# Routed experts of a transformer block: fp32 matmuls become three fp32r products with split weights

## The reference

```python
scores = sigmoid(x @ router_weight.T)
topk_indices = _get_topk_indices(scores, e_bias)      # best 2 groups of 4, then best 2 experts
combine = zeros((T, 16)).at[arange(T)[:, None], topk_indices].add(topk_weights)
h1 = einsum('th,ehi->tei', x, w_up)                   # 512 -> 256, each expert
a = relu2(h1) * combine[:, :, None]                   # relu(h) squared
routed = einsum('tei,eih->th', a, w_down)             # 256 -> 512
shared = relu2(hidden @ shared_up) @ shared_down
```

## Time and profile before

| | us |
|---|---|
| median of 3 runs (2376.22 to 2377.37) | 2376.26 |
| profiled execution | 2383.18 |
| its span | 2381.4 |
| PE busy | 1936.1 (81%) |
| PEld busy | 1183.5 (50%) |
| DVE busy | 1152.1 (48%) |
| ACT busy | 761.1 (32%) |
| POOL busy | 610.8 (26%) |

### The profile page before, as it was taken

How to read it: one execution, slowest core, us unless ns; L and a number is a source line. 1 busy time by engine, 2 the same in 40 slices (tenths; PEclk the granted TensorE clock), 3 DMA queues, 4 the chain that set the end, 5 groups by cost and what they waited for, 6 DMA issues and landing times. The chain is left out here.

```text
span 2381.4 us, 34828 instructions
## 1 busy us (share of the span) xinstructions
PE 1936.1 (81%) x9788; PEld 1183.5 (50%) x9789; DVE 1152.1 (48%) x2951; ACT 761.1 (32%) x1215; POOL 610.8 (26%) x743
## 2 busy tenths in 40 slices
PE   4888887888887888887888876999999759999900
PEld 0644433644434544435544324767777636666600
DVE  3355544345643455633556528555555223333358
ACT  1345452245452255533344513222222112222200
POOL 0201116111125011143011144554444421000064
PEclk8889998899998899998799997999999979999955
DMA  6222203222302222312322223222222186333388
GB/s 212 54 54 54 50 23 99 53 54 54 72 5 95 54 54 54 72 46 79 64 44 43 56 92 121 97 94 93 84 84 89 66 309 229 127 128 128 113 296 309
DMA packets 104973, 232.52 MB, mean 98 GB/s; under 512 B 20440, under 2 KB 20440, under 8 KB 104812
## 3 DMA queue, kind: packets, MB, share of 16 engines
q1 hardware_dynamic: 81008, 171.86, 25.2%
q0 software_dynamic: 14848, 50.34, 5.8%
q10 hardware_dynamic: 8960, 8.41, 1.1%
HBM read 113.06 MB, written 67.17 MB: 76 GB/s over the span
## 5 line engine op out<-in xcount | busy, mean ns | idle before, releaser
L402 ACT ACTIVATE pr<-sc 128x1024 f32<-128x1024 f32 (+3 forms) x384 | 307.9, 811 | 263.2 <-PE sc L641 261.3
L661 PE MATMUL O<-pr,V 128*32 128x512 f32 (+3 forms) x3072 | 325.6, 498 | 42.6 <-ACT oD L414 42.6
L328 POOL TENSOR_SCALAR_AFFINE_SELECT pr<-pr 128x256 f32<-128x256 f32 x256 | 103.4, 409 | 969.7 <-ACT pr L402 969.7
L504 DVE TENSOR_REDUCE mx<-ring 128x1 f32<-128x512 f32 x256 | 169.6, 678 | 246.2 <-PE ring L616 244.5
L500 DVE CUSTOM_DVE_ANT_0 ring<-ring,mask 128x512 f32<-128x512 f32 (+3 forms) x512 | 240.8, 511 | 62.7 <-PE ring L616 60.4
L641 PE MATMUL sc<-stk 128*128 128x512 f32 (+3 forms) x768 | 241.6, 396 | 23.0 <-ACT pr L402 20.9
L641 PEld LDWEIGHTS sc<-stk 128*128 128x128 f32 x768 | 115.7, 189 | 262.5 <-ACT pr L402 155.3
L616 PE MATMUL ring<-stk 96*128 96x512 f32 (+3 forms) x768 | 218.0, 388 | 20.0 <-DMA stk<-st 13.1
L616 PEld LDWEIGHTS ring<-stk 96*128 96x128 f32 x768 | 144.6, 204 | 68.2 <-DVE mx L500 17.6
L529 DVE RECIPROCAL oD<-oD 128x128 f32<-128x128 f32 x128 | 117.6, 934 | 93.1 <-ACT oD L414 93.1
L1519 PE MATMUL ue<-wu_e,xT_e 128*128 x632 | 151.2, 383 | 0.1
(11 more groups left out here) (228 smaller groups left out, 3396.1 us busy)
## 6 DMA issues: line engine op xcount, KB each, us to landing
stk<-st SPq DMA_DIRECT2D x192, 256.0 KB, 5.0
x_e<-xs SPq DMA_DIRECT2D x79, 256.0 KB, 2.6
ys<-y_e SPq DMA_DIRECT2D x79, 256.0 KB, 2.0
oT<-in_L_attn_x_dram ACTq DMA_DIRECT2D x16, 512.0 KB, 5.6
st<-in_L_attn_x_dram SPq DMA_DIRECT2D x32, 256.0 KB, 3.2
x1d<-pr SPq DMA_DIRECT2D x32, 256.0 KB, 2.1
xb<-x1d SPq DMA_DIRECT2D x32, 256.0 KB, 2.9
part<-y_sh SPq DMA_DIRECT2D x32, 256.0 KB, 2.0
```

The source lines that it names most:

```text
L402: nc.scalar.activation(pr[:, g % PRB, :, off:], sc[g % 2][:, :, off:], ACT.Exp, scale=SCALE).then_inc(exp_done, 1)
L504: nc.vector.tensor_reduce(mx[:, heads[0]:heads[-1] + 1, qt, part], bank[:, 0:len(heads) * w].rearrange("p (e k) -> p e k", e=len(heads)), ...
L661: last = nc.tensor.matmul(O[row:row + 32, off:], V[:, col:col + DH], pr[:, g % PRB, e, off:], start=(i == 0), stop=(i == 4 * c + 3))
```

## The change

The expert stage goes from plain fp32 to the three-pass product. GpSimd now fetches an expert's weights into one of three raw buffers, copies them rounded to fp32r into one of eight places (`WR`), and subtracts to get the low part; hi and lo lie next to each other, so that one up matmul of 512 columns gives x_hi times both, and one of 256 columns adds x_lo times w_hi. The ninth and later experts wait for their place by the count of finished tiles (`endi`). ScalarE makes the high parts and now also copies the cross term and the result; VectorE makes the low parts, adds the cross term, and does relu and square in one instruction. The wait for the weights moves from TensorE to VectorE, which loads the expert's count once a tile, with its check. TensorE loads an offset (`eslot`) without a check; the loop's first two rounds of four load two, the other two load one. Spare tiles now ask for expert 15 instead of expert 0. In the loads of the first three experts nothing waits for the zero rows any more.

```diff
+WR = 8
+RAW = 3
-        xT = sb("xT_e", [P, 2, KC, P])
+        xhi, xlo = sb("xhi_e", [P, 2, KC, P], f32r), sb("xlo_e", [P, 2, KC, P], f32r)
...
+            def split(e):
...
+                pool.wait_ge(raw_in[z], (e // RAW + 1) * 32)
+                if e >= WR:
+                    done = pool.value_load(endi[0:1, e - WR:e - WR + 1], min_val=1, max_val=NET + 1)
+                    pool.wait_ge(d_done, done)
+                    apart(pool)
+                nc.gpsimd.tensor_copy(up[:, :, 0, :], up_raw).then_inc(whi_ready, 1)
+                nc.gpsimd.tensor_copy(dn[:, :, 0, :], dn_raw).then_inc(whi_ready, 1)
+                pool.wait_ge(whi_ready, 2 * e + 2)
+                nc.gpsimd.tensor_tensor(up[:, :, 1, :], up_raw, up[:, :, 0, :].bitcast(f32), ALU.subtract).then_inc(w_ready, 1)
+                nc.gpsimd.tensor_tensor(dn[:, :, 1, :], dn_raw, dn[:, :, 0, :].bitcast(f32), ALU.subtract).then_inc(w_ready, 1)
+            for e in range(RAW):
+                fetch(e)
+            for e in range(E):
+                if e == WR:
+                    pool.wait_ge(tables, 1)
+                split(e)
+                if e + RAW < E:
+                    pool.wait_ge(w_ready, 2 * e + 2)
+                    fetch(e + RAW)
...
         @block.scalar
...
-                    nc.scalar.activation(r[:, s % 2, :], ub[s % 2][:, 0:EI], ACT.Relu).then_inc(r_ready, 1)
+                    nc.scalar.activation(cross[:, s % 2, :], ub[s % 2][:, EI:2 * EI], ACT.Copy).then_inc(cross_ready, 1)
+                if has(j + 1 if known(j) else j):
...
+                    nc.scalar.activation(ahi[:, (s + 1) % 2, :, :], tab[(s + 1) % 2][:, 0:EC * P].rearrange("p (k t) -> p k t", k=EC), ACT.Copy).then_inc(ahi_ready, 1)
+                if has(j):
...
+                    nc.scalar.activation(y[:, s, :], db[s % 2][:, :], ACT.Copy).then_inc(y_ready, 1)
...
         @block.vector
...
+                if has(j + 3 if known(j) else j):
+                    split = dve.value_load(eid[0:1, j + 3:j + 4] if known(j) else eid[0:1, bass.ds(j + 3, 1)], min_val=2, max_val=2 * E)
+                    dve.wait_ge(w_ready, split)
+                    apart(dve)
+                    dve.wait_ge(xhi_ready, j + 4)
+                    nc.vector.tensor_tensor(xlo[:, z, :, :], txb[z][:, :, :], xhi[:, z, :, :].bitcast(f32), ALU.subtract).then_inc(xlo_ready, 1)
+                    nc.vector.tensor_tensor(h1[:, :], ub[s % 2][:, 0:EI], cross[:, s % 2, :], ALU.add).then_inc(h1_ready, 1)
+                    nc.vector.scalar_tensor_tensor(a[:, s % 2, :], h1[:, :], 0.0, h1[:, :], ALU.max, ALU.mult).then_inc(a_ready, 1)
+                    nc.vector.tensor_tensor(alo[:, z, :, :], tab[z][:, 0:EC * P].rearrange("p (k t) -> p k t", k=EC),
+                                            ahi[:, z, :, :].bitcast(f32), ALU.subtract).then_inc(alo_ready, 1)
...
         @block.tensor
...
-                return pe.value_load(K.eid[0:1, t:t + 1] if known(t) else K.eid[0:1, bass.ds(t, 1)], min_val=0, max_val=E - 1)
+                return nc.values_load(at, engines=[mybir.EngineType.PE], min_val=0, max_val=(WR - 1) * SLOT,
+                                      skip_runtime_bounds_check_because="the table holds multiples of SLOT below WR * SLOT")
+                if has(j + 2 if known(j) else j):
+                    slot[s + 2] = offset(j + 2)
+                    w = slot[s + 2]
+                if has(j):
+                    w_down = slot[s] if s >= 2 else offset(j)
-                    e = expert(j + 2)
-                    pe.wait_ge(w_ready, e + 1)
-                        last = nc.tensor.matmul(ub[s % 2][:, 0:EI], xT[:, s % 2, k, :], K.wu[:, bass.ds(e * (KC * EI) + k * EI, EI)],
-                                                start=(k == 0), stop=(k == KC - 1))
+                        both = lambda: nc.tensor.matmul(ub[s % 2][:, :], xhi[:, s % 2, k, :], part(wup, at, 2 * EI, w),
+                                                        start=(k == 0), stop=(k == KC - 1), skip_group_check=True)
+                        if k < KC - 1:
+                            both()
+                        nc.tensor.matmul(ub[s % 2][:, 0:EI], xlo[:, s % 2, k, :], part(wup, at, EI, w),
+                                         start=False, stop=False, skip_group_check=True)
+                        if k == KC - 1:
+                            last = both()
-                    for k in range(EC):
-                        last = nc.tensor.matmul(db[s % 2][:, :], aT[:, s % 2, k, :], K.wd[:, bass.ds(e * (EC * D) + k * D, D)],
-                                                start=(k == 0), stop=(k == EC - 1))
+                    terms = [(a_, h, k) for k in range(EC) for a_, h in ((ahi, 0), (ahi, 1), (alo, 0))]
+                    for n, (a_, h, k) in enumerate(terms):
+                        last = nc.tensor.matmul(db[s % 2][:, :], a_[:, s % 2, k, :], part(wdn, (2 * k + h) * D, D, w_down),
+                                                start=(n == 0), stop=(n == len(terms) - 1))
```

More of the change, by code:

```diff
@@ L1290, in expert_phase @@
         sem = lambda n: ctx.enter_context(nc.semaphore(n))
+        wup = sb("wup_e", [P, WR * KC * 2 * EI], f32r)
+        wdn = sb("wdn_e", [P, WR * EC * 2 * D], f32r)
+        raw = sb("raw_e", [P, RAW, WN])
         x = sb("x_e", [P, XR, D])
-        xT = sb("xT_e", [P, 2, KC, P])
-        r = sb("r_e", [P, 2, EI])
+        xhi, xlo = sb("xhi_e", [P, 2, KC, P], f32r), sb("xlo_e", [P, 2, KC, P], f32r)
+        cross = sb("cross_e", [P, 2, EI])
+        h1 = sb("h1_e", [P, EI])
         a = sb("a_e", [P, 2, EI])
-        aT = sb("aT_e", [P, 2, EC, P])
+        ahi, alo = sb("ahi_e", [P, 2, EC, P], f32r), sb("alo_e", [P, 2, EC, P], f32r)
         y = sb("y_e", [P, XR, D])
@@ L1313, in expert_phase @@
         base = sb("base", [P, E])
-        inside, other, mine_e = sb("inside", [P, E]), sb("other", [P, E]), sb("mine_e", [P, E])
-        rowf = sb("rowf", [P, 4])
+        inside, other = sb("inside", [P, E]), sb("other", [P, E])
+        rowf = sb("rowf", [P, 6])
         padf = sb("padf", [P, E])
@@ L1319, in expert_phase @@
         moved = sb("moved", [P, 2 * NTILE])
-        padi = sb("padi", [P, E], i32)
+        padi, endi = sb("padi", [P, E], i32), sb("endi", [P, E], i32)
+        eid, eslot, xrow = sb("eid", [P, NET], i32), sb("eslot", [P, NET], i32), sb("xrow", [P, NET], i32)
         iotas, zeroed, step, tables = sem("iotas"), sem("rows_zeroed"), sem("table_step"), sem("tables")
         in_columns, in_rows = sem("in_columns"), sem("in_rows")
-        w_in = [sem(f"we_in{i}") for i in range(2)]
-        w_ready, padded = sem("we_ready"), sem("padded")
+        raw_in = [sem(f"raw_e_in{i}") for i in range(RAW)]
+        whi_ready, w_ready, padded = sem("whi_e_ready"), sem("we_ready"), sem("padded")
         block = ctx.enter_context(nc.Block())
@@ L1464, in _ @@
             nc.vector.tensor_copy(padi[:, :], padf[:, :])
+            nc.vector.tensor_scalar(endi[:, :], ends[:, :], float(PRIMED), None, ALU.add)
             ts(inside[:, :], starts[:, :], jf[:, 0:1], None, ALU.is_le)
@@ L1468, in _ @@
             then(tt(inside[:, :], inside[:, :], other[:, :], ALU.subtract))
-            red(rowf[:, 0:1], inside[:, :], AX.X, ALU.add)
-            tt(other[:, :], inside[:, :], base[:, :], ALU.mult)
-            then(tt(mine_e[:, :], inside[:, :], ef[:, :], ALU.mult))
+            red(rowf[:, 2:3], other[:, :], AX.X, ALU.add)
+            then(red(rowf[:, 0:1], inside[:, :], AX.X, ALU.add))
+            then(ts(rowf[:, 2:3], rowf[:, 2:3], float(E - 1), None, ALU.min))
+            then(tt(other[:, :], inside[:, :], base[:, :], ALU.mult))
             red(rowf[:, 1:2], other[:, :], AX.X, ALU.add)
-            red(rowf[:, 2:3], mine_e[:, :], AX.X, ALU.add)
+            then(ts(rowf[:, 4:5], rowf[:, 2:3], float(WR), -float(WR), ALU.is_ge, ALU.mult))
+            then(tt(rowf[:, 4:5], rowf[:, 4:5], rowf[:, 2:3], ALU.add))
+            ts(rowf[:, 4:5], rowf[:, 4:5], float(SLOT), None, ALU.mult)
+            then(ts(rowf[:, 2:3], rowf[:, 2:3], 2.0, 2.0, ALU.mult, ALU.add))
             then(ts(rowf[:, 3:4], jf[:, :], float(P), None, ALU.mult))
@@ L1496, in _ @@
             pe.wait_ge(in_columns, 1)
-            for n in range(2):
+            for n in range(3):
                 last = nc.tensor.transpose(txb[0][0:1, n, 0:NET], rowf[0:NET, 2 + n:3 + n], K.ident[0:NET, 0:NET])
@@ L1500, in _, with offset, part @@
             pe.wait_ge(tables, 1)
-            def expert(t):
-                return pe.value_load(K.eid[0:1, t:t + 1] if known(t) else K.eid[0:1, bass.ds(t, 1)], min_val=0, max_val=E - 1)
-            def round_(j, s):
+            slot = {}
+            def offset(t):
+                at = eslot[0:1, t:t + 1] if known(t) else eslot[0:1, bass.ds(t, 1)]
+                return nc.values_load(at, engines=[mybir.EngineType.PE], min_val=0, max_val=(WR - 1) * SLOT,
```

(10 more changed lines are left out.)

87 lines of the change are left out of this document (44 added, 43 removed).

## The result

The changed kernel takes 2339.95 us (median of six runs, 2338.48 to 2341.45) against 2376.62 (2375.71 to 2377.92) for the kernel before beside it: ratio 0.9846, 95% interval 0.9833 to 0.9858, 36.7 us less. The forecast was 2331, range 2319 to 2354. The profiled execution took 2338.48 us, its span is 2336.7.

A forecast was written before the change was run, and what follows sets the result against it. TensorE's expert round was taken as the bound; 43.6 us from shorter rounds and 2 from the start took the profiled 2383.18 to 2337.6, or the 2376.26 median to 2330.7 us. Range 2319 to 2354.

The forecast's parts named there:

- The bound and the round: Expert stage: TensorE stays the bound, its round falls from 4.11 to 3.55 us, 42.8 us over 76 full rounds.
- the prediction's own signs: Signs of being right: TensorE rounds of 3.5 to 3.6 us without idle time, expert stage 284 us instead of 329.
- rival D: TensorE's fp32r matmuls run at column count alone: round 3.25 us, gain 68, 2308 us; chance 0.04.
- rivals A and B: TensorE's sequencer binds: A, round 3.83 us, 2353 us, chance 0.13; B, round 4.70, slower at 2421 us, chance 0.10.
- 1.8 us to spare: Expert rounds: ScalarE's and VectorE's results are ready some 1.8 us before TensorE wants them.
- rival C: VectorE's wait for weights near tile 7, GpSimd needing 15 us an expert: 2346 us; chance 0.06.
- Weights: GpSimd's splits take 9.5 us an expert and stay hidden: cost 0, at most 1 to 2 us at tile 7.
- The start: Expert stage's beginning: fewer weights beside the first x and a shorter ramp, net gain 2 us, bounds -1 and +5.
- The table's delay: Start of the expert stage: extra table steps on VectorE, a transpose and a cast make it 1.2 us later.
- the forecast's own: Whole kernel: the forecast's own range, 2320 to 2342 us, from round 3.44 to 3.69 and start -1 to +5; chance 0.67.

The follow-up runs named there:

- e_loads: Changed kernel with two checked register loads of the offset per tile on TensorE instead of one or two unchecked: 2348.58 us, ratio 0.9883.
- e_best2: Changed kernel with weight wait on TensorE, no VectorE load, ReLU on ScalarE, zero rows on two queues, fourth expert fetched later: 2327.81 us, ratio 0.9794.
- e_copies: Changed kernel with GpSimd making the weights' low parts by a second copy instead of a subtraction (values wrong): 2347.15 us, ratio 0.9851.

## Why the prediction was right, and where it was off

- **The bound and the round.** Right in kind: TensorE stays full, the round shrinks at each part. 3.46 us instead of the forecast 3.55: transposes in front of fp32r, 512 columns and the first product behind transposes came as taken from the earlier trace rows. Off were two small terms: 256 columns cost 0.12 and not 0.1275, and the two transposes 0.13 and not half of four (0.18). Over 76 rounds this is 6 to 7 us more gain; 2.7 of it went to what VectorE loses beside GpSimd. By the prediction's own signs the round lies just under its 3.5 to 3.6 us, and from first transposes to last down matmul the stage takes 280.8 us (forecast 284).
- **Fp32r at its column count alone (rival D)** fell: 512 columns cost 0.23.
- **TensorE's sequencer (rivals A and B)** fell: late rounds have no idle time, and with two checked loads a tile they are still 3.46. By e_loads such loads cost 3.4 us in ramp and rounds together and not 0.3 us a round. Only in e_best2 do steady rounds show them.
- **ScalarE and VectorE.** The forecast 1.8 us to spare held but for rounds beside GpSimd's splits, early and near 2090 us: TensorE's weight loads waited 1.6 us in all, six times, for the stretched square. The prediction called itself wrong if TensorE waited for VectorE at all in full rounds; it did, for this little. That the two engines disturb each other was thought of only for GpSimd's time (rival C), not for VectorE's.
- **Weights.** Right: they are never waited for. The copy, taken as 1.5 between bounds 1.05 and 2.34, is 1.04 or 1.05 us in most cases and at most 1.27; the subtraction 2.33 to 2.63, with 3.39 and 3.32 for the first expert. An expert takes 8.5 to 9.0 us and not 9.5. Rival C fell.
- **The start** was the step that failed, in sign and outside its bounds: forecast a gain of 2 (bounds -1 and +5), measured a loss of 4.6. The prediction looked at the weights beside the first x, and not at the weights beside the zero rows, whose landing must be complete before x is issued; its term for that was nothing. The kernel before held the third expert back until the zero rows had landed, as its timeline shows:

```profile
1927.79 0.78 POOL L1401 DMA_DIRECT2D wu_e<-in_L_ffn_w_up_dram  x1 [22.86 <-DMA xs<-zero_rows]
```

The changed kernel has no such wait: it fetches three experts at once, a fourth at 1924.27 and a fifth at 1932.79. So the sixteen issues took 1.5 us more, and x was issued 6.4 us behind the last of them instead of 2.4, 4.0 more. The table's delay came as forecast (issue 9.2 us after the stage's start, 7.7 before), the ramp from first transposes to the fourth too (8.5; 8 forecast, 9.8 before), and the first x took 4.0 us instead of 4.8 to land.
- **Attention** had no term at all. The prediction took stages that the diff does not touch as unchanged; with the VectorE load attention was 6.5 us longer.
- **The sum** in medians: forecast -45.6. Rounds -46.5 (forecast -43.6), start +4.6 (forecast -2), attention +6.5 (forecast 0): -35.4, measured -36.7. The forecast missed by 9 us: start and attention together by 13.1, of which the rounds gave back 2.9 and the rest 1.3. The measured time lies in the stated range and even in the forecast's own (2320 to 2342; by its bounds, round 3.69 and start -1, the upper end is 2344.6). Neither range has a term for attention or for a start this late, so that they held it is in part luck.

## What to carry to other kernels

Price a matmul stream part by part from the same kernel's starts: that gave the round within 3%. Then look at the edges, which cost more than the stream's error: what transfers run beside the ones that gate the first tile, and how many issues one queue must make before it. And compare also the stages that the change does not touch; a register load in one loop can lengthen another.

## What the runs showed of the hardware

- VectorE with both operands in SBUF was stretched from 0.42 to 2.14 us (at most 2.64) beside GpSimd's two-operand subtraction and to 2.07 (at most 2.33) beside its copies (e_copies), and ended 0.26 to 0.30 us behind GpSimd's instruction; with one operand in PSUM it stayed at 0.42.
- GpSimd copied 128x1024 from fp32 to fp32r in 1.04 us and subtracted in 2.33, beside VectorE's work in up to 1.27 and 2.63, and in 3.3 to 3.4 beside VectorE's small table work.
- A checked VectorE register load in the expert loop moved VectorE's idle time at attention's loop turns ahead of the normalisation, and TensorE's wait for it rose from 64 to 66 us to 71 to 73; an empty instruction at its program's head did neither.
- Sixteen register-addressed DMA issues took 17.1 to 18.6 us on one queue and 10.8 on two.
